# A transformer layer on one core: the first three feed-forward weight units quantized during the attention, and the last attention products placed between the first gate and up products

## The chip, the cores and the metric

The kernel runs on one core of a Trainium2 chip. The metric is the device time of one execution in microseconds (us), lower is better. The engines are called by the names of the profile: PE (TensorE), DVE (VectorE), ACT (ScalarE), POOL (GpSimd) and SP (SyncE, which here only starts transfers).

## What is computed

One pre-norm layer on 2048 tokens of width 1024, float32 in and out. First `x = x + attention(layernorm(x))`, where the attention mixes the 32 heads of each token with one another (scores are 32 x 32 for every token, not across tokens). Then `x = x + ffn(layernorm(x))`:

```
q, k, v = (h @ w.T + b).reshape(B, S, 32, 32)        # for wq, wk, wv
scores = einsum('bshd,bstd->bsht', q, k) / sqrt(32)
context = einsum('bsht,bstd->bshd', softmax(scores), v)
...
dq = NF4_CODE[searchsorted(bounds, w / absmax)] * absmax   # blocks of 64, for w1, w2, w3
h = silu(x @ dq1.T) * (x @ dq2.T)
return h @ dq3.T                                     # w1, w2: 2752 x 1024; w3: 1024 x 2752
```

So every feed-forward weight is rounded to one of 16 levels of its block of 64 before it is used, and that rounding is computed in the kernel.

## The kernel before

**Stages.** A first stage (to about 62 us) turns the three projection weights and splits them into a high and a low float16 part. The attention then takes the tokens in 16 tiles of 128, one `step` each (n = 0 to 15; steps 2 to 13 run in a loop of two). Step n projects tile n (`project_one`, 96 products of 512 columns on PE) and, between these, does the small products of tile n-1: 32 scores (`score_part`, L1048) and 32 products with V (`mix_part`, L1061), each against a block-diagonal stationary matrix, `q_diag` or `p_diag`. ACT fills these matrices (`place`, L934), DVE does the softmax, transposes and evacuations, POOL the residual, the reciprocal roots and the low halves. The normalized result of tile n-2 is split in two float16 halves (`halve2`, `low2`), transposed by DMA (`turn_high2`, `turn_low2`) and stored. Beside this DVE looks at all of w1, w2, w3 (`look_at`) for the largest value of each block of 64. `tail` finishes tile 15, whose scores and context have no projection left to hide behind.

**Feed-forward.** 22 tiles of the hidden dimension go in 11 rounds of two. A round first makes gate and up products (`gate_up`, tile p = 0 and 1, four blocks `sb_` of 512 tokens each, 24 products each for gate and for up), then 16 `down` tiles of 12 products. It needs six weight units of 128 x 1024; unit v of a round is UNIT[v], so the first six are w1 tile 0, w2 tile 0, w1 tile 1, w2 tile 1, w3 tile 0, w3 tile 1. A unit costs a division by the block maxima (POOL, `divide` L1378), 14 comparisons (ACT, `compare` L1497, into a ring of int8 signs), 14 multiply-adds (DVE, `sum_steps` L1633, in PSUM banks 0 and 1), a fifteenth comparison and two more passes on POOL (`step_apart`, `times_absmax`), the high half (ACT, `high_half` L1520), the low half (POOL, `low_half` L1410), and two DMA transposes (`turn` L1310). Between its sums DVE also makes the hidden values (`hidden_value` L1659) and adds the down products (`add_down` L1712). Three units are ahead at any time. The order on each engine is written out by hand; each engine runs its instructions in that order and waits at semaphores.

**The passage.** The feed-forward programs are generators. In the last step and in `tail` the attention program of each engine calls `next(feed)` at chosen places and so puts pieces of the opening of the feed-forward between its own. Before the change units 0 and 1 are made here in another way: ACT and DVE compare against the 15 bounds (`early_signs` L1508, `early_compares` L1643), and PE adds the results up by products with diagonal matrices of the level steps (`early_sums` L1861, 4 products for each of 15 levels and 2 units, with the scores and the context of tile 15 put between them); POOL makes these matrices (L1472), and DVE scales the sums (`early_codes` L1650). Unit 2 goes the usual way through DVE. The first gate product (L1804, which waits for unit 0) comes when all of that is done:

```
            early_sums(0, 0, 2)
            score = yield
            early_sums(0, 2, 7, score)
            early_sums(0, 7, LEVELS)
            early_sums(1, 0, 5)
            mix = yield
            early_sums(1, 5, 10, mix)
            early_sums(1, 10, LEVELS)
            yield
            pe.wait_ge(rounded, EARLY + 1)
            rounds(pe, body)
```

The x2 tokens that the gate products read are loaded back from DRAM (`load_tokens`, L1340) in blocks of 512; block 3 holds tiles 12 to 15.

## Time and profile before

| | |
|---|---|
| median of 3 runs | 1966.15 us (1963.84 to 1967.97) |
| profiled execution | 1965.0 us |
| its span, first to last instruction | 1963.1 us |
| mean granted TensorE clock | 0.995 |
| PE busy | 1911.5 us, 97% |
| DVE busy | 1738.3 us, 89% |
| ACT busy | 1477.6 us, 75% |
| POOL busy | 1192.4 us, 61% |
| first score product / end of the last projection | 90.1 us / 549.0 us |
| first gate product | 598.5 us |

Busy time is summed over an engine's instructions; the matmuls are pipelined, so each is shown longer (0.38 us) than the distance to the next. The idle time of an engine stands in square brackets, with what ended it. The profiled execution took 1.9 us more than its span.

### The profile page before, as it was taken

How to read it: one execution, taken by the hardware profiler on the slowest of the kernel's cores; microseconds unless marked ns; L12 is line 12 of the kernel's file. 1: busy time of each engine (PE TensorE's matmuls, PEld its weight loads, DVE VectorE, ACT ScalarE, POOL GpSimd, SP SyncE). 2: the span in 40 equal slices, each digit the busy share in tenths (PEclk: the TensorE clock that was granted, in tenths of full speed). 3: DMA queues.
4: the chain of work that ended last, by engine and by line, in shares of the span. 5: the costliest groups of instructions: out<-in, count | busy, mean ns of one | idle time of the engine just before them, and what ended most of it. 6: DMA issues, size and time to landing. Idle time of an engine off the chain costs nothing. (4 is left out here: it accounts for less than half of the span.)

```text
span 1963.1 us, 31165 instructions
## 1 busy us (share of the span) xinstructions
PE 1911.5 (97%) x10444; PEld 1062.7 (54%) x10444; DVE 1738.3 (89%) x1853; ACT 1477.6 (75%) x1672; POOL 1192.4 (61%) x715
## 2 busy tenths in 40 slices
PE   6899999999988989999999999999999999999998
PEld 6588888888854434444444444444444444444443
DVE  6788888888887999999999999999999999999982
ACT  7253443534486979899898998989989889898883
POOL 0211211112146787787887978879788797786975
PEclk9999999999999999999999999999999999999999
DMA  9335555455348512121221221212212212122114
GB/s 311 108 108 172 160 156 185 142 169 155 92 150 241 177 45 58 44 64 43 48 59 43 52 55 43 64 43 48 59 43 55 52 43 64 43 46 57 38 28 183
DMA packets 253803, 183.78 MB, mean 94 GB/s; under 512 B 177840, under 2 KB 220848, under 8 KB 253744
## 3 DMA queue, kind: packets, MB, share of 16 engines
q1 hardware_dynamic: 220144, 168.33, 30.6%
q10 hardware_dynamic: 33600, 14.69, 3.0%
q8 instruction: 34, 0.56, 0.1%
q14 instruction: 25, 0.20, 0.0%
HBM read 115.34 MB, written 25.17 MB: 72 GB/s over the span
## 5 line engine op out<-in xcount | busy, mean ns | idle before, releaser
L1633 DVE SCALAR_TENSOR_TENSOR bank<-signs,bank 128x1024 f32<-128x1024 int8 (+2 forms) x761 | 926.5, 1217 | 53.4 <-ACT signs L1497 25.6
L1497 ACT ACTIVATE signs<-w_nat,compare_bias 128x1024 int8<-128x1024 f32 (+2 forms) x896 | 959.1, 1133 | 5.3 <-POOL w_nat L1378 3.0
L1804 PE MATMUL bank<-x2T_hi,w12T_hi 128*128 128x512 f16 x1376 | 522.1, 379 | 7.7 <-DMA w12T_lo<-half 5.1
L1806 PE MATMUL bank<-x2T_hi,w12T_lo 128*128 128x512 f16 x1376 | 522.3, 380 | 0.0
L1805 PE MATMUL bank<-x2T_lo,w12T_hi 128*128 128x512 f16 x1376 | 522.2, 379 | 0.0
L1020 PE MATMUL bank<-wT_hi,xT_hi 128*128 128x512 f16 x768 | 293.2, 382 | 2.4 <-PEq L325 2.4
L1020 PE MATMUL bank<-wT_hi,xT_lo 128*128 128x512 f16 x768 | 293.1, 382 | 0.0
L1831 PE MATMUL bank<-w3T_hi,hT_hi 128*128 128x512 f16 x672 | 255.3, 380 | 8.9 <-DMA w3T_lo<-half 3.7
L1833 PE MATMUL bank<-w3T_hi,hT_lo 128*128 128x512 f16 x672 | 255.5, 380 | 0.0
L1832 PE MATMUL bank<-w3T_lo,hT_hi 128*128 128x512 f16 x672 | 255.4, 380 | 0.0
L1423 POOL TENSOR_TENSOR acc<-acc,hidden 128x512 f32<-128x512 f32 x176 | 221.0, 1271 | 39.8 <-ACT hidden L1546 39.0
L1390 POOL TENSOR_SCALAR step_part<-w_nat 128x1024 f32<-128x1024 f32 (+1 forms) x64 | 230.5, 3602 | 14.3 <-POOL w_nat L1403 7.4
L1804 PEld LDWEIGHTS bank<-x2T_hi,w12T_hi 128*128 128x128 f16 x1376 | 134.8, 98 | 171.5 <-issue 3.7
L1806 PEld LDWEIGHTS bank<-x2T_hi,w12T_lo 128*128 128x128 f16 x1376 | 134.7, 98 | 162.7 <-issue 0.7
L1805 PEld LDWEIGHTS bank<-x2T_lo,w12T_hi 128*128 128x128 f16 x1376 | 134.8, 98 | 162.5 <-issue 0.8
L1399 POOL TENSOR_TENSOR w_nat<-w_nat,step_part 128x1024 f32<-128x1024 f32 (+1 forms) x64 | 149.8, 2341 | 103.2 <-DVE w_nat L1633 103.2
L1546 ACT ACTIVATE hidden<-bank,un_scale 128x512 f32<-128x512 f32 x176 | 120.2, 683 | 112.0 <-PE bank L1833 66.1
L972 ACT ACTIVATE probs<-probs 128x512 f32<-128x512 f32 x32 | 20.2, 630 | 218.5 <-DVE probs L877 218.1
L1069 PEld LDWEIGHTS bank<-vT,p_diag 128*128 128x128 f32 x1024 | 169.0, 191 | 14.8
L1057 PEld LDWEIGHTS bank<-kT,q_diag 128*128 128x128 f32 x1024 | 169.0, 191 | 14.7
L1712 DVE SCALAR_TENSOR_TENSOR acc<-bank,un_scale,acc 128x512 f32<-128x512 f32 x176 | 131.3, 746 | 33.8 <-PE bank L1829 22.6
L1410 POOL TENSOR_TENSOR half<-w_nat,half 128x1024 f16<-128x1024 f32 (+1 forms) x66 | 139.7, 2116 | 29.7 <-ACT half L1520 29.7
(143 smaller groups left out, 2596.8 us busy)
## 6 DMA issues: line engine op xcount, KB each, us to landing
ff_raw<-in_L_ffn_w SPq DMA_DIRECT2D x63, 512.0 KB, 4.1
w_nat<-in_L_ffn_w SPq DMA_DIRECT2D x63, 512.0 KB, 3.9
x_nat<-in_L_attn_hidden_states SPq DMA_DIRECT2D x16, 512.0 KB, 5.0
x_res<-in_L_attn_hidden_states SPq DMA_DIRECT2D x16, 512.0 KB, 4.4
x<-x_res SPq DMA_DIRECT2D x16, 512.0 KB, 3.9
acc<-x SPq DMA_DIRECT2D x4, 2048.0 KB, 8.3
out<-acc SPq DMA_DIRECT2D x16, 512.0 KB, 2.7
w_raw<-in_L_attn_wq SPq DMA_DIRECT2D x8, 512.0 KB, 7.1
```

The source lines that it names most:

```text
L1020: ins = nc.tensor.matmul(to, x, w, start=j == 0, stop=j == len(passes) - 1)
L1057: ins = nc.tensor.matmul(scores[:, t], q_diag[:, t], kT[:, t // 2, :, t % 2], start=True, stop=True)
L1390: nc.gpsimd.tensor_scalar(step_part[0:rows, 0:cols], w_nat[0:rows, slot, 0:cols], float(BOUNDS[APART]), 2 * HALF_STEP[APART], ALU.is_gt, A ...
L1423: nc.gpsimd.tensor_tensor(acc[:, st, BANK:], acc[:, st, BANK:], hidden[:, st % 2], ALU.add).then_inc(summed, 1)
L1497: nc.scalar.activation(signs[0:rows, ring(v, k), 0:cols], w_nat[0:rows, v % SLOTS, 0:cols], ACT.Sign, scale=COMPARE[SUMMED[k]][0], bias=co ...
L1633: V.scalar_tensor_tensor(to, part, HALF_STEP[SUMMED[k]], before, ALU.mult, ALU.add).then_inc(sign_used, 1)
L1804: nc.tensor.matmul(dst, hi, x2T_hi[:, toks, c], start=c == 0, stop=False)
L1805: nc.tensor.matmul(dst, hi, x2T_lo[:, toks, c], start=False, stop=False)
L1806: last = nc.tensor.matmul(dst, lo, x2T_hi[:, toks, c], start=False, stop=c == C - 1)
L1831: nc.tensor.matmul(dst, hT_hi[k, p, toks], w3T_hi[k, p, cols], start=p == 0, stop=False)
L1832: nc.tensor.matmul(dst, hT_hi[k, p, toks], w3T_lo[k, p, cols], start=False, stop=False)
L1833: last = nc.tensor.matmul(dst, hT_lo[k, p, toks], w3T_hi[k, p, cols], start=False, stop=p == GROUP - 1)
```

## The change

It makes units 0, 1 and 2 during steps 1 to 15, three of the 45 levels in each: POOL divides a unit once (`open_unit`), ACT compares and scales (`make_level`: two activations), POOL adds (`add_level`). PE and DVE have no part in it. To make room the two block-diagonal matrices become one (`diag`, halves of which hold q and the probabilities in turn), `qkv` becomes one row buffer, and the halves of the weights get a buffer of their own from the start. In the last step POOL and ACT scale and split units 0 and 1, and unit 2 in the tail. All of `early_signs`, `early_compares`, `early_sums`, `early_codes`, the diagonal matrices and DVE's sums for unit 2 go. DVE's work on the scales (`look_at_scales`, `set_scales`, the reciprocals) moves from the last step and the tail to the end of step 14 and into step 15. PE goes on from the last projection with the first gate products; the scores of tile 15 sit one behind each of products 0 to 31, its context behind products 40 to 71 (of 96: gate of block 0, gate of block 1, up of block 0, up of block 1), in PSUM banks 6 and 7. Tiles 14 and 15 of x2 are transposed straight into place instead of going through DRAM. ACT and POOL no longer loop over the steps. Unit 3's sums are spread over DVE's tail.

```
-            for diag in (q_diag, p_diag):
-                pool.memset(diag[:], 0.0).then_inc(diag_zero, 1)
+            pool.memset(diag[:], 0.0).then_inc(diag_zero, 1)
...
+            def add_level(n, i):
+                at = (n - 1) * STEP_LEVELS + i
+                v, k = divmod(at, LEVELS)
+                if k > 0:
+                    pool.wait_ge(level_ready, at + 1)
+                    ...
+                    nc.gpsimd.tensor_tensor(codes[v], codes[v], level, ALU.add).then_inc(level_added, 1)
...
+            def make_level(n, i):
+                ...
+                if adds_before(at) > 0:
+                    act.wait_ge(level_added, adds_before(at))
+                nc.scalar.activation(level, ratio, ACT.Sign, scale=COMPARE[k][0], bias=compare_bias[:, k:k + 1]).then_inc(level_sign, 1)
+                act.wait_ge(level_sign, at + 1)
+                nc.scalar.activation(codes[v] if k == 0 else level, level, ACT.Copy, scale=HALF_STEP[k]).then_inc(level_ready, 1)
...
@@ attention, scalar, step @@
                 if attend:
+                    make_level(n, 0)
                     exponential(n, 0)
                     place_probs(n, 0, end)
...
                     place_probs(n, 1, end)
...
+                if attend:
+                    make_level(n, 1)
                 if project:
-                    place(q_diag, qT[:].rearrange("p t h u -> p t u h"), q_placed)
+                    place_q(n, 0, attend)
...
+                if attend:
+                    make_level(n, 2)
+                if project:
+                    place_q(n, 1, attend)
...
@@ attention, gpsimd, step @@
                 if end:
                     residual(n - 2)
+                if feed:
+                    next(feed)
                 if normalize:
                     inv_std(pool, n + 1)
                 if end:
                     inv_std2(n - 2)
+                if attend:
+                    add_level(n, 0)
                 if feed:
                     next(feed)
                 if end:
                     low2(n - 2)
+                if attend:
+                    add_level(n, 1)
                 if feed:
                     next(feed)
+                if attend:
+                    add_level(n, 2)
+                if n * STEP_LEVELS % LEVELS == 0 and n + 1 < T:
+                    open_unit(n * STEP_LEVELS // LEVELS)
+                if ahead:
+                    next(ahead)
...
@@ attention, vector, tail @@
                 evacuate(T - 1, 1, None, 2, 1)
                 turn_v(T)
+                moments2(T - 2)
                 next(feed)
                 center(T, 0)
+                norm2(T - 2)
+                flip_probs(T, 0, True)
+                next(feed)
                 center(T, 1)
...
@@ attention, sync, tail @@
                 sp.wait_ge(projected, 6 * T)
+                next(feed)
                 sp.wait_ge(evacuated, 6 * T)
-                sp.wait_ge(x2_out, 32 * (T - ST_BLOCK + 1))
                 next(feed)
                 store_x1(T - 2)
...
+            def turn_tokens(n):
+                sp.wait_ge(x2_hi_done, n + 1)
+                sp.dma_start_transpose(x2T_hi[:, n], x2_half[:]).then_inc(x2_turned, 16)
+                sp.wait_ge(x2_lo_done, n + 1)
+                sp.dma_start_transpose(x2T_lo[:, n], x2_low).then_inc(x2_turned, 16)
...
+                        for at, (m, sb_) in enumerate(((0, 0), (0, 1), (1, 0), (1, 1))):
+                            gate_up(r, 0, sb_, P, (m,), True, 3 * C * at)
...
+                def attend_last(slot):
+                    if slot < QUAD:
+                        score_part(T, True, slot, slot + 1)
+                    elif MIX_FROM <= slot < MIX_FROM + QUAD:
+                        mix_part(T, slot - MIX_FROM, slot - MIX_FROM + 1)
```

DVE's pieces of the feed-forward, in their new order (step 14's end; then five places in step 15; then the tail): `look_at_scales`; `floor_scales`; `set_scales`; `first_reciprocals`, `scale_absmax`; `invert(2, 11)`; `invert(11, 22)`; sum 0; sums 1 to 3; sum 4; sums 5 and 6; sums 7 to 9; `hidden_value(0, 0, 0)` and sums 10 and 11; `hidden_value(0, 0, 1)`; sums 12 to 15. POOL's in step 15: the square root of the scales; `early_times(0)`, `early_times(1)`, `early_low(0)`, `early_low(1)`; `divide(0, 3)`. ACT's: `early_high(0)`, `early_high(1)` between `place_probs(15, 0)` and the second exponential. SP loads block 0 of the x2 tokens in step 15, behind the transposes and the store of tile 13, and blocks 1 and 2 at the two waits of its tail. `place_q(n, half)` waits for the context of the same half (`context_done`), since both use `diag`.

## Rows read from the trace of the kernel before

**Rows 1.** The page: busy time of the engines, and GpSimd over forty slices.

```profile
PE 1911.5 (97%) x10444; PEld 1062.7 (54%) x10444; DVE 1738.3 (89%) x1853; ACT 1477.6 (75%) x1672; POOL 1192.4 (61%) x715
...
POOL 0211211112146787787887978879788797786975
```

**Rows 2.** Timeline, PE, 549 to 703: start, us, line, work, idle before.

```profile
556.27 1.01 PE L1861 MATMUL bank<-w3T_hi,w12T_hi 128*128 128x512 f16 x2 [7.31 <-issue]
...
598.49 0.39 PE L1804 MATMUL bank<-x2T_hi,w12T_hi 128*128 128x512 f16 x1 [2.63 <-DVE w_nat L1650]
...
650.49 0.39 PE L1804 MATMUL bank<-x2T_hi,w12T_hi 128*128 128x512 f16 x1 [2.64 <-DMA w12T_lo<-half]
...
702.36 0.39 PE L1831 MATMUL bank<-w3T_hi,hT_hi 128*128 128x512 f16 x1 [3.69 <-DVE acc L1712]
```

**Rows 3.** Windows of PE: us, busy (count), granted clock, DMA share, GB/s.

```profile
555.00:560.00 5.00, 3.73 (x12) 0.57 1.05 398
```

**Rows 4.** Timeline of a looped attention step (starts 427.35, next 458.00), PE, ACT, DVE, POOL.

```profile
427.35 0.30 PE L1057 MATMUL bank<-kT,q_diag 128*128 128x32 f32 x2
...
458.00 0.30 PE L1057 MATMUL bank<-kT,q_diag 128*128 128x32 f32 x2
...
473.77 0.30 PE L1069 MATMUL bank<-vT,p_diag 128*128 128x32 f32 x2
...
479.48 0.30 PE L1069 MATMUL bank<-vT,p_diag 128*128 128x32 f32 x2
...
477.25 1.26 ACT L937 ACTIVATE p_diag<-flipped 32x512 f32<-32x512 f32 x2
...
466.58 0.80 DVE L279 TENSOR_SCALAR x_nat<-x_nat,mean_var,rstd 128x1024 f32<-128x1024 f32 x1
...
464.72 0.55 POOL L721 TENSOR_TENSOR rstd<-var_eps,power 128x1 f32<-128x1 f32 x1 [1.20 <-DVE var_eps L267]
```

**Rows 5.** Groups by line: name, shapes, count, busy us, mean ns.

```profile
L1399 POOL TENSOR_TENSOR w_nat<-w_nat,step_part 128x1024 f32<-128x1024 f32 x61 | 143.9, 2358 | 96.3 <-DVE w_nat L1633 96.3
...
L937 ACT ACTIVATE p_diag<-flipped 32x512 f32<-32x512 f32 x128 | 80.3, 628 | 50.1 <-DVE flipped L892 29.7 <-issue 19.3
...
L1520 ACT ACTIVATE half<-w_nat 128x1024 f16<-128x1024 f32 x63 | 66.1, 1050 | 10.1 <-DVE w_nat L1650 5.3 <-POOL w_nat L1403 4.8
...
L1508 ACT ACTIVATE hT_hi<-w_nat,compare_bias 128x1024 f16<-128x1024 f32 x7 | 7.7, 1133 | 0.0
```

**Rows 6.** Timeline around 582.5, DVE and POOL.

```profile
582.67 2.41 DVE L883 TENSOR_SCALAR x_res<-x_res,mean_var,rstd 128x1024 f32<-128x1024 f32 x1
...
582.41 2.13 POOL L1410 TENSOR_TENSOR half<-w_nat,half 128x1024 f16<-128x1024 f32 x1 [4.55 <-ACT half L1520]
```

**Rows 7.** Timeline, DVE: the two long reciprocals.

```profile
548.62 2.52 DVE L1678 RECIPROCAL inv_absmax<-inv_absmax 128x384 f32<-128x384 f32 x1
...
588.64 3.75 DVE L1678 RECIPROCAL inv_absmax<-inv_absmax 128x576 f32<-128x576 f32 x1
```

**Rows 8.** DMA issues: KB each, median us from issue to landing.

```profile
x<-x_res SPq DMA_DIRECT2D x16, 512.0 KB, 3.9
...
x2T_lo<-x_lo_dram SPq DMA_DIRECT2D x4, 1024.0 KB, 8.4
...
w12T_lo<-half SPq DMA_TRANSPOSE x44, 3.1
```

**Rows 9.** Timeline, POOL and DVE, 601 to 702.

```profile
601.67 2.38 POOL L717 TENSOR_TENSOR x_res<-x_res,flipped 128x1024 f32<-128x1024 f32 x1 [5.67 <-DMA x_res<-in_L_attn_hidden_states]
...
609.59 0.81 DVE L883 TENSOR_SCALAR x_res<-x_res,mean_var,rstd 128x1024 f32<-128x1024 f32 x1 [2.53 <-DMA x<-x_res]
...
648.68 0.75 DVE L1659 SCALAR_TENSOR_TENSOR hidden<-bank,un_scale,hidden 128x512 f32<-128x512 f32 x1 [1.15 <-ACT hidden L1528]
...
701.56 0.74 DVE L1712 SCALAR_TENSOR_TENSOR acc<-bank,un_scale,acc 128x512 f32<-128x512 f32 x1
```

**Rows 10.** Windows of all engines: PE, PEld, DVE, ACT, POOL busy (count).

```profile
760.00:800.00 40.00, 40.00 (x187) 18.19 (x186) 38.93 (x35) 38.12 (x41) 30.55 (x16) 1.00 0.23 53
```

571 lines of the change are left out of this document (284 added, 287 removed).

## The prediction, made before the result was seen

> **What bounds the kernel now.** I read the page first. PE is busy for 97% of the span [rows 1], so only two things can shorten the kernel: PE work that goes, and the stretches in which PE waits. POOL's slices are at 0 to 2 tenths up to the feed-forward [rows 1]: that is the room which the change uses. The timeline of PE then shows where it waits. It runs without a gap through the attention to 549.0 us, sits idle for 7.3 us to 556.3, and starts the first gate product at 598.5 [rows 2]. Between lie the 120 summing products and tile 15's scores and context. After that come, among shorter ones, waits of 2.6 and 3.7 us [rows 2], and further on none: in a 40 us window of a later round PE has 187 products, one per 0.214 us, and DVE is busy for 38.9 of the 40 [rows 10]. So from the first down products on PE and DVE are nearly equal, and neither can make up time; what the passage gains or loses stays to the end. The wait at 702.4 has DVE behind it [rows 2]: at that point DVE is the later one. From the fourth hidden value (648.68) to the first addition of a down product (701.56) DVE runs 38 sums and four hidden values with hardly a gap, 52.9 us [rows 9]. The change touches none of these. Small pieces that have no row of their own (a softmax step, a transpose, an issue) are my estimates from the same timeline. I cost the change as the shift of that fourth hidden value, `hidden_value(0, 0, 3)`. It needs the up product of token block 3, thus the x2 of tile 15, and the DVE work ahead of it.
>
> **Attention steps 1 to 14.** Each gets two ScalarE activations per level, 1.13 us (Sign, with a 16-bit output) and 1.05 us (Copy) [rows 5], three times: 6.6 us, and three POOL additions of 2.36 us [rows 5]: 7.1 us. Both engines have that room. What matters is the order. The second half of the probabilities is in place at 477.25 + 1.26 = 478.5, and PE reads it at 479.5 [rows 4]: 1.0 us of slack. No new ACT work stands ahead of it after the step's beginning. But the first `add_level` follows the reciprocal root of 464.72 + 0.55 = 465.3 and runs to 467.6, over the x normalization on DVE at 466.58, which takes 0.80 us alone [rows 4]. Such an instruction suffers: the x2 normalization at 582.67 took 2.41 us while POOL worked from 582.41 to 584.54, and ended 0.5 us after it [rows 6], against 0.81 us in [rows 9]. The Trainium skill (GPSIMD Reference, section 1, Specifications) states that VectorE instructions in a two-port mode or with two SBUF inputs contend with GpSimd; the row agrees for the first kind, and no row of the second kind is used here. So the normalization ends at 468.2 instead of 467.4, everything behind it on DVE and ACT comes 0.8 us later, and 0.2 us of slack is left: no wait, taken as 0, though closely. The bound below is 0. The one above is an addition that starts just before the normalization: 2.36 + 0.5 - 0.80 = 2.1 us late, less 1.0 us slack, 1.1 us for each of 14 steps, 15 us.
>
> The single `diag` forces an order: q of the next tile can be placed only when the context of the same half is done. The first half is done at 479.5, the second at 485.2. A half takes 4 x 0.63 = 2.5 us [rows 5], with 2.2 us of `make_level` before each: first half at about 484, second at about 490. PE's steps start 30.7 us apart (427.35, 458.00), so it wants them at 488.7 and 5.7 us later, at 494.4. Slack 4 us: cost 0. One buffer for q, k and v changes no order on DVE: 0. The missing `memset` and the shorter first stage are off PE's path: 0. Straight instead of looped code on ACT and POOL: between 0 and a few tenths of a microsecond per step, taken as 0, since nothing on these engines is late by less than the slack.
>
> **Step 15.** Here DVE gets more: `set_scales` with its small operations (2 us), `scale_absmax` (1 us), the two reciprocals of 2.5 and 3.75 us [rows 7], and `look_at_scales` moves ahead of the step. By the order of the code the reduction over partitions on POOL now comes before tile 13's residual, and both before the centring: the first half of the probabilities comes about 3 us late. The second half has `set_scales`, `early_high` twice on ACT, and three DVE operations held by POOL's `early_times` and `early_low` (2 us each, back to back) before it: about 6 us more. I add 9 us: PE's projections end at 558 instead of 549. Bounds: 0 and 12.
>
> **The start of the gate products.** They need unit 0 (split and transposed by about 546, hidden) and token block 0. SP issues its load behind tile 13's transposes and store, at about 550.5, and the low half, issued half a microsecond behind the high one, lands 8.4 us later [rows 8]: 559.4, taken as 559.5. So of the 9 us of step 15 only 1.5 us count, the rest lies beside the load, as PE's idle 7.3 us do now. A wait that long also costs clock: the granted clock was 0.57 in 555 to 560 [rows 3]; with the shorter waits I take no loss (bound above 2 us).
>
> **The opening.** 24 products take 5.2 us; a small product behind each adds (479.48 - 473.77) / 16 - 0.214 = 0.14 us [rows 4], 9.2 us for all 64, which were also done before. Undisturbed, the context of tile 15 would be done 25 us after 559.5. Two waits come in. The x2 normalization of tile 14 stands before `flip_probs` on DVE and waits for `store_x1(14)`, which SP issues at 563.6 (by the 13 us that DVE's added work and waits put on tile 14's transpose, 548 before), behind the loads of blocks 1 and 2: about 8 us to landing in place of 3.9 [rows 8], the same queue as a block load. That makes the first half of the probabilities 3 us late (ready 576), the second 1.5 us more, with sums 1 to 4 ahead of it on DVE. Context done: 588.8. Then the chain of the last tile: weighing and transpose 2 us, residual 2.4, and from its end to the normalization 5.5 us as in [rows 9] (604.05 to 609.59, the store that must land); normalization 0.8, high half 1.05 [rows 5], low half 2.1 [rows 6], issue and DMA transpose 1.2 + 3.1 [rows 8]: 588.8 + 18.1 = 606.9. The roundtrip through DRAM that followed is gone. PE meanwhile: last up product 594, block 2 604.4, then a wait of 2.5 us, block 3 until 617.3; silu and hidden value: 618. DVE has then finished sums 0 to 15 of unit 3 and 4 and eight more (by 613), since unit 2's 14 sums, ten comparisons and two scalings left it; it is no later than PE.
>
> **The sum.** 648.7 - 618.0 = 30.7 us earlier. The waits before the down products come again as they are, since the same DVE chain sets them. 1965.0 - 30.7 = 1934.3 us for the profiled execution; the median of the runs was 1.15 us above that execution, so 1935.5, rounded to 1935 us. The own range of this case is 1924 (nothing in step 15 and the store at 3.9 us: 10 us less) to 1944 (12 us in step 15, clock lost, store and last chain 3 us later each).
>
> **Rivals.** (1) POOL holds DVE in every step, the bound above: 1935 + 15 = 1950. For it speaks the 0.2 us of slack; against it that the addition starts 1.3 us before the normalization [rows 4], so most of it is over. Any lateness of 0.5 us per step already gives 1942. Chance 0.2, 1944 to 1956. (2) DVE isn't the bound of the passage, so that PE's own work sets the end: from 598.5 to its last product PE has about 1343 us of products besides its waits; 559.5 + 9.2 + 1343 + 8 to the end of the execution gives 1920. For it speaks that DVE loses some 35 us of work in the tail; against it the gapless 52.9 us of [rows 9]. Chance 0.13. (3) Slower: the shared `diag`. If ACT's chain from the context to q (two `make_level`, each waiting for POOL, then the placing) runs over its slack of 4 us, PE stands at the scores of each step. It decides from 30.7 / 14 = 2.2 us per step beyond the slack, so 6 us more than I count; at 9 us more it would be 1935 + 70 = 2005. Chance 0.04. (4) The early units are not what held the gate products, and tile 15's chain alone keeps the end within 0.2%: the fourth hidden value would have to stay at 645 to 652, which only a wait of 30 us could do. Chance 0.02.
>
> **Numbers.** Forecast 0.61, rivals 0.2, 0.13, 0.04 and 0.02. About 0.2% of the time (4 us) is what a measurement of this kernel can tell from no change. Faster than that: 0.61 + 0.2 + 0.13 = 0.94; within 0.02; slower 0.04. The range that leaves out no more than 2 in 10 reaches to most of both faster rivals: 1920 to 1951.
>
> **What would show it.** Right: no wait of PE in steps 1 to 14 and the same distance of 30.7 us between their starts; waits of some us before the context products of step 15; first gate product near 559, its releaser the token load; `hidden_value(0, 0, 3)` near 618; 52.9 us from there to the first addition; 187 products per 40 us later. Wrong: idle time on PE before score or context products of each step with ACT's placing as releaser (rivals 1 and 3); a gate product before 552; a distance to the first addition below 50 us (rival 2).

## The result and the profile after

The changed kernel takes 1948.17 us (median of 4 runs, 1946.46 to 1950.49), the kernel before 1964.99 us (4 runs, 1961.58 to 1967.97): ratio 0.9917, 95% interval 0.9905 to 0.993. The forecast was 1935 us within 1920 to 1951. The sign is right and the range holds it, but about 13 us of the expected 30 did not come. The profiled execution took 1950.5 us (span 1948.4, against 1963.1 before).

In these texts, lines of code after the change are those of the changed kernel; `L1154` is the context product (before: L1069), `L1883` gate and up, `L1002` the placing into `diag`, `L766` `add_level`, `L772` the residual addition, `L949` the x2 normalization, `L1788` `add_down`.

PE's waits first, as in [rows 2] (timeline of PE, 540 to 690: start, length, line, work, idle before and what ended it):

```profile
544.58 0.60 PE L1154 MATMUL bank<-vT,diag 128*128 128x32 f32 x2 [10.51 <-ACT diag L1002]
...
555.97 0.64 PE L1154 MATMUL bank<-vT,diag 128*128 128x32 f32 x2 [3.34 <-ACT diag L1002]
...
571.82 0.39 PE L1883 MATMUL bank<-x2T,w12T 128*128 128x512 f16 x1 [3.45 <-DMA x2T<-x_lo_dram]
...
589.36 0.38 PE L1154 MATMUL bank<-vT,diag 128*128 128x32 f32 x2 [2.34 <-ACT diag L1002]
...
636.81 3.65 PE L1883 MATMUL bank<-x2T,w12T 128*128 128x512 f16 x10 [2.65 <-DMA w12T<-half]
...
687.14 0.61 PE L1911 MATMUL bank<-w3T_hi,hT_hi 128*128 128x512 f16 x1 [3.72 <-DVE acc L1788]
```

The first gate product is at 571.82, where it was at 598.49; the forecast had 559.5. Ahead of it stand two waits in step 15, 13.9 us together, and one for the token load. Around them the clock is low: the granted clock was 0.50, which is the level of 1.2 GHz, in the 5 us around the first wait, and 0.57 around the second (windows of all engines; the number behind POOL's is the clock, then DMA share and GB/s):

```profile
540.00:545.00 5.00, 0.42 (x3) 0.46 (x4) 4.83 (x11) 3.06 (x5) 3.89 (x2) 0.50 0.00 0
...
555.00:560.00 5.00, 4.04 (x18) 3.59 (x19) 4.96 (x6) 4.91 (x7) 1.75 (x1) 0.57 1.05 211
```

Up to step 14 everything went as forecast. DVE's x normalization starts beside a level addition and takes 1.58 us, 0.8 more than in [rows 4], and no wait of PE follows (DVE, then POOL, in the looped step):

```profile
466.33 1.58 DVE L276 TENSOR_SCALAR x_nat<-x_nat,mean_var,rstd 128x1024 f32<-128x1024 f32 x1
...
465.00 2.37 POOL L766 TENSOR_TENSOR codes<-codes,w12T 128x1024 f32<-128x1024 f32 x1
```

The trouble begins behind step 14, on POOL (timeline of POOL, 516 to 550):

```profile
516.79 2.38 POOL L766 TENSOR_TENSOR codes<-codes,w12T 128x1024 f32<-128x1024 f32 x1 [2.52 <-ACT w12T L1045]
524.89 0.39 POOL L1568 PARTITION_ALL_REDUCE top_all<-top  x1 [5.72 <-issue]
532.38 2.37 POOL L772 TENSOR_TENSOR x_res<-x_res,flipped 128x1024 f32<-128x1024 f32 x1 [7.11 <-issue]
534.72 0.59 POOL L1571 TENSOR_TENSOR top_all<-pow,power 128x1 f32<-128x1 f32 x1
...
541.11 4.21 POOL L1556 TENSOR_TENSOR w12T<-w12T,inv_first 128x1024 f32<-128x1024 f32 x2 [1.56 <-DVE inv_first L1778]
```

The reduction over the partitions itself takes 0.39 us. But POOL stands for 5.72 us ahead of it and for 7.11 us behind it, "issue", that is, for nothing that the profile shows. Before the change the residual addition of tile 13 was at 518.45 and the reduction at 529.32, with 7.44 us of the same stand behind it, beside other work. Now `ahead` puts the reduction first, so the residual addition comes 13.9 us later, and DVE stands for it, with the centring of the scores queued behind. The stand ahead of the reduction is not all lost: its input, DVE's `top`, is ready only at 521.92, so 3.0 us of the 5.72 lie behind that. What POOL does in the two stands no run shows. (Timeline of DVE:)

```profile
521.74 0.18 DVE L1750 TENSOR_REDUCE top<-ff_raw 128x1 f32<-128x22 f32 x1
...
534.78 1.29 DVE L258 BATCH_NORM_STATS2 stats<-x_res 128x6 f32<-128x512 f32 x2 [9.30 <-POOL x_res L772]
...
541.14 0.71 DVE L958 STREAM_TRANSPOSE flipped<-probs 128x512 f32<-128x512 f32 x1
...
546.86 5.85 DVE L1782 TENSOR_SCALAR absmax<-absmax,w_scale 128x352 f32<-128x352 f32 x3
552.64 0.70 DVE L958 STREAM_TRANSPOSE flipped<-probs 128x512 f32<-128x512 f32 x1
...
584.87 0.81 DVE L949 TENSOR_SCALAR x_res<-x_res,norm_row 128x1024 f32<-128x1024 f32 x1 [4.06 <-DMA x<-x_res]
```

The second flip stands behind `scale_absmax`, three instructions that took 0.40 us each before and 5.85 us together here, beside POOL's `early_low` and `low2`.

The stands delay the codes of units 0 and 1 as well: the root, which the scales need, is at 534.72, the multiplication at 541.11, and unit 0's low half ends at 548.15. The token load follows from that (timeline of POOL, 545 to 548, then SP's queue, 548 to 574):

```profile
545.59 2.56 POOL L1560 TENSOR_TENSOR x_nat<-w12T,x_nat 128x1024 f16<-128x1024 f32 x1 [0.28 <-ACT x_nat L1606]
```

```profile
548.24 0.33 SPq L1362 DMA_DIRECT2D w_nat<-in_L_ffn_w  x1
548.69 3.35 SPq L1425 DMA_TRANSPOSE w12T<-x_nat  x2
...
555.84 2.66 SPq L1425 DMA_TRANSPOSE w12T<-x_nat  x2
...
560.83 0.92 SPq L1416 DMA_DIRECT2D x2T<-x_hi_dram  x1
561.80 1.11 SPq L1416 DMA_DIRECT2D x2T<-x_lo_dram  x1
...
573.62 0.35 SPq L701 DMA_DIRECT2D x<-x_res  x1
```

SP waits until 548.2 for the low half of unit 0 (12.8 us in the list of its waits, ended by POOL's L1560). It also waits for the projections of q, but these had ended at 530.3, and those of k, which the token load needs, end at 552.3. From 548.2 it issues thirteen transfers in one piece, and the token load of block 0 is the last of them, at 560.83 where the forecast had 550.5. So neither of PE's two waits in step 15 holds the token load; the late codes do.

Later on: the fourth hidden value is at 632.35 (forecast 618, before 648.68 [rows 9]) and the first addition of a down product at 686.34 (before 701.56), 54.0 us later:

```profile
632.35 0.75 DVE L1735 SCALAR_TENSOR_TENSOR hidden<-bank,un_scale,hidden 128x512 f32<-128x512 f32 x1 [3.03 <-ACT hidden L1624]
...
686.34 0.74 DVE L1788 SCALAR_TENSOR_TENSOR acc<-bank,un_scale,acc 128x512 f32<-128x512 f32 x1
```

The rounds behind are as they were, 187 products in 40 us [rows 10]; the busy line of the page shows the 120 summing products gone and ACT and POOL fuller [rows 1]:

```profile
PE 1892.1 (97%) x10324; PEld 1058.0 (54%) x10324; DVE 1722.9 (88%) x1833; ACT 1552.3 (80%) x1792; POOL 1277.0 (66%) x724
```

```profile
760.00:800.00 40.00, 40.00 (x187) 18.13 (x186) 38.84 (x35) 36.88 (x40) 27.93 (x14) 1.00 0.24 54
```

### The profile page after: what moved, and what is told of

It reads as the page before. It is cut to its first block, busy times and chain, and to the rows that moved or that the text cites. A ratio compares the mean times of both kernels' runs of the same rounds, so it can differ in the third digit from the quotient of the medians.

```text
span 1948.4 us, 30908 instructions
## 1 busy us (share of the span) xinstructions
PE 1892.1 (97%) x10324; PEld 1058.0 (54%) x10324; DVE 1722.9 (88%) x1833; ACT 1552.3 (80%) x1792; POOL 1277.0 (66%) x724
## 4 chain that ended last, share of the span: by engine, by line
PE 64%; DVE 0%; issue 0%; ACT 0%; DMA 0%; POOLq 0%; SPq 0%; POOL 0%; DVEq 0%
PE bank L1883 41%; PE bank L1911 7%; PE bank L1912 7%; PE bank L1913 7%; PE bank L1909 0%; PE bank L1908 0%; DVE bank L1727 0%; DMA w3T_lo<-half 0%; ACT hidden L1642 0%; POOLq L154 0%; DVE bank L1725 0%; DVE w_nat L1727 0%; SPq L1386 0%; ACT half L1614 0%; ACT signs L1601 0%
## 5 line engine op out<-in xcount | busy, mean ns | idle before, releaser
L1883 PE MATMUL bank<-x2T,w12T 128*128 128x512 f16 x4128 | 906.4, 380 | 6.6 <-DMA x2T<-x_lo_dram 3.5
L1883 PEld LDWEIGHTS bank<-x2T,w12T 128*128 128x128 f16 x4128 | 410.3, 99 | 488.0 <-DMA x2T<-x_lo_dram 3.9
L1481 POOL TENSOR_SCALAR step_part<-w_nat 128x1024 f32<-128x1024 f32 (+2 forms) x63 | 226.9, 3601 | 10.6 <-POOL w_nat L1494 7.4
L1490 POOL TENSOR_TENSOR w_nat<-w_nat,step_part 128x1024 f32<-128x1024 f32 (+2 forms) x63 | 147.5, 2341 | 91.9 <-DVE w_nat L1727 91.8
L1154 PEld LDWEIGHTS bank<-vT,diag 128*128 128x128 f32 x1024 | 175.7, 196 | 33.4 <-issue 13.8
L1142 PEld LDWEIGHTS bank<-kT,diag 128*128 128x128 f32 x1024 | 171.6, 192 | 15.2
L1154 PE MATMUL bank<-vT,diag 128*128 128x32 f32 x1024 | 159.5, 238 | 16.2 <-ACT diag L1002 16.2
L1788 DVE SCALAR_TENSOR_TENSOR acc<-bank,un_scale,acc 128x512 f32<-128x512 f32 x176 | 131.4, 747 | 34.2 <-PE bank L1909 22.5
L1142 PE MATMUL bank<-kT,diag 128*128 128x32 f32 x1024 | 156.5, 234 | 0.0
L1501 POOL TENSOR_TENSOR half<-w_nat,half 128x1024 f16<-128x1024 f32 (+2 forms) x63 | 133.3, 2116 | 25.1 <-ACT half L1616 25.1
L1104 PEld LDWEIGHTS bank<-wT_hi,xT_lo 128*128 128x128 f16 x768 | 115.3, 150 | 31.3 <-issue 1.6
```

What stands on the lines that cost most here:

```text
L1104: ins = nc.tensor.matmul(to, x, w, start=j == 0, stop=j == len(passes) - 1)
L1142: ins = nc.tensor.matmul(scores_of(n)[:, t], diag[:, t], kT[:, t // 2, :, t % 2], start=True, stop=True)
L1154: ins = nc.tensor.matmul(context_of(n)[:, t], diag[:, t], vT[:, t // 2, :, t % 2], start=True, stop=True)
L1481: nc.gpsimd.tensor_scalar(step_part[0:rows, 0:cols], w_nat[0:rows, slot, 0:cols], float(BOUNDS[APART]), 2 * HALF_STEP[APART], ALU.is_gt, A ...
L1490: nc.gpsimd.tensor_tensor(w_nat[0:rows, slot, 0:cols], w_nat[0:rows, slot, 0:cols], step_part[0:rows, 0:cols], ALU.add).then_inc(step_adde ...
L1883: last = nc.tensor.matmul(dst, w, x[:, toks, c], start=c == 0 and i == 0, stop=c == C - 1 and i == 2)
```

## The experiments

All start from the changed kernel. Each profile's clock starts at a slightly different point of the execution, so times of different kernels are compared as distances from one row, the moments of x on DVE in step 13 (L258, `stats<-x_nat`, at 460.84 in the changed kernel). "Turn", "gate" and "addition" are the distances from there of SP's issue of unit 0's transposes, of the first gate product and of the first `add_down`. The runs were made in five sets, in which the kernel before had medians of 1962.9 to 1965.0 us, so between sets a difference of medians below some 2 us says nothing; the distances do not have this fault.

| kernel | time, us | context waits of step 15 | wait for the gate | turn | gate | addition |
|---|---|---|---|---|---|---|
| changed | 1948.2 | 10.5 + 3.3 | 3.5 | 87.9 | 111.0 | 225.5 |
| e1, reduction is a copy | 1939.5 | 0.3 + 5.4 | 3.0 | 77.6 | 100.4 | 215.1 |
| e2, reduction twice | 1947.3 | 11.0 + 3.5 | 3.4 | 88.4 | 111.3 | 225.8 |
| e3, scaling later | 1949.3 | 10.3 + 0 | 9.8 | 87.7 | 110.4 | 224.1 |
| e4, normalization later | 1947.4 | 10.0 + 3.2 | 3.1 | 87.3 | 110.3 | 224.0 |
| e5, tokens of block 0 first | 1949.7 | 10.2 + 2.2 | 0 | 93.4 | 103.9 | 228.9 |
| e6, no levels | 1962.7 | 6.5 + 3.1 | 4.7 | 83.9 | 106.7 | 220.6 |
| e7, reduction behind the residual | 1952.5 | 0 + 0 | 28.0 | 94.1 | 116.2 | 229.9 |
| e9, store ahead of tokens | 1942.8 | 10.2 + 2.2 | 6.4 | 87.5 | 110.4 | 220.7 |
| e12, both chains | 1944.2 | 0 + 0 | 18.5 | 84.7 | 106.6 | 220.9 |
| e13, both chains, tokens | 1941.8 | 0 + 0 | 8.8 | 84.7 | 97.0 | 218.6 |
| e14, levels of 8 columns | 1942.8 | 6.7 + 3.1 | 4.8 | 84.0 | 106.9 | 219.5 |
| e16, and hidden value first | 1939.7 | 0 + 0 | 8.4 | 84.7 | 96.5 | 217.8 |

Wherever SP's order up to the tokens of block 0 is that of the changed kernel (all but e5, e13 and e16), the gate comes 21.9 to 23.1 us behind the turn, whatever PE waited for in step 15.

**Is it the stand of POOL?**

```diff
-            nc.gpsimd.partition_all_reduce(top_all[:], top[:], P, ALL_MAX).then_inc(ff_max_all, 1)
+            nc.gpsimd.tensor_copy(top_all[:], top[:]).then_inc(ff_max_all, 1)
```

> The maximum over the partitions, which GpSimd takes at the end of step 14, is replaced by a plain copy of the same tile on GpSimd (this leaves out that maximum, so the scales of the first two units are those of each partition's own rows). Theory, that GpSimd stands for about 7 us between the reduction and its next ordinary instruction: the residual addition of block 13 starts about 7 us and more earlier (now 532.4, then near 523 to 525), VectorE's idle stretch of 9.3 us ahead of the row centring is gone, TensorE's wait of 10.5 us at 544.6 shrinks to under 3, and the time is about 1938 to 1941 us (ratio to the kernel before about 0.987). Rival, that the wait is VectorE's and ScalarE's added load of step 15 (inversions, scales, high halves): the residual addition moves, but the wait at 544.6 keeps 6 us or more and the time stays above 1944.

Measured: 1939.5 us (1938.47 to 1940.09), ratio 0.9883 (0.9867 to 0.99). Both stands are gone (timeline of POOL):

```profile
520.24 0.19 POOL L1568 COPY top_all<-top 128x4 f32<-128x4 f32 x1 [2.81 <-DVE top L1750]
520.38 2.40 POOL L772 TENSOR_TENSOR x_res<-x_res,flipped 128x1024 f32<-128x1024 f32 x1
```

The residual addition starts 10.3 us earlier by distance, the first wait is gone, and the first gate product comes 10.6 us earlier, as the turn of unit 0 comes 10.2 us earlier. The second wait grew to 5.4 us: PE, at full clock, reaches it sooner, and the 5.85 us of the scaling are still there. The theory's time was right. This puts 8.7 us on the reduction and its stands by the medians, 6.7 by the ratios to the kernel before, and 10.4 at the first addition.

**How often does POOL stand?**

```diff
+            nc.gpsimd.partition_all_reduce(top_all[:], top[:], P, ALL_MAX).then_inc(ff_first_all, 1)
+            pool.wait_ge(ff_first_all, 1)
             nc.gpsimd.partition_all_reduce(top_all[:], top[:], P, ALL_MAX).then_inc(ff_max_all, 1)
```

> The maximum over the partitions is taken twice in a row on GpSimd, same result. If the pause of about 7 us belongs to each such reduction, residual addition of block 13 starts 12 to 14 us later than in the changed kernel (near 545) and the time rises by about 12, to 1960. If the pause belongs to the return from a reduction to ordinary instructions, only the second reduction's own time is added, some 1 to 6 us, and the time rises by no more than that. Rival, that GpSimd's pause does not set TensorE's wait: the time does not move.

Measured: 1947.31 us (1945.97 to 1949.24), as the changed kernel.

```profile
523.86 0.39 POOL L1569 PARTITION_ALL_REDUCE top_all<-top  x1 [5.78 <-issue]
524.34 0.37 POOL L1571 PARTITION_ALL_REDUCE top_all<-top  x1
531.82 2.36 POOL L772 TENSOR_TENSOR x_res<-x_res,flipped 128x1024 f32<-128x1024 f32 x1 [7.10 <-issue]
```

The second reduction starts 0.48 us after the first. So the price is at the changes, from ordinary instructions to the reduction and back, and not in the reduction: two in a row pay it once. The time alone doesn't separate this from the rival, which had no change either; e1 does.

**The second wait alone.**

```diff
             first_reciprocals()
-            scale_absmax()
             yield
             invert(2, FT // 2)
+            scale_absmax()
```

> One instruction group is moved: VectorE's scaling of the maxima (three instructions, 5.85 us in the changed kernel, 0.40 us each in the kernel before) goes behind the flips of the second half of the probabilities and the second inversion. Theory, that its 5.85 us are all that makes the wait of 3.34 us at 556.0, and that GpSimd's running additions, not the scaling itself, make them: the wait is gone, the three instructions take another time where they stand now, and the kernel gains 2 to 3.5 us (about 1945.5). Rival, that the inversion behind it is held in its place, since whatever stands there meets the same additions: the wait stays above 2 us and the time is that of the changed kernel.

Measured: 1949.34 us (1946.28 to 1950.61), no gain. The wait is gone, as the theory had it; the three instructions took 4.07 us in their new place, so they are held there as well. But the gate starts only 0.6 us earlier by distance, and PE's wait there grew from 3.5 to 9.8 us. Both the theory's gain and the rival's mechanism were wrong: the wait was real and did not matter. PE's projections end 6.9 us earlier by distance, but the turn of unit 0 and the token load behind it stay where they were.

**Both waits, by order alone.** POOL does the residual addition and the standard deviation of tile 13 ahead of the reduction; DVE's scales and ACT's high halves go behind the scores' work. In POOL's step:

```diff
                 if end:
                     residual(n - 2)
-                if feed:
-                    next(feed)
                 if normalize:
                     inv_std(pool, n + 1)
                 if end:
                     inv_std2(n - 2)
+                if feed:
+                    next(feed)
+                    next(feed)
                 if attend:
                     add_level(n, 0)
...
-                if ahead:
-                    next(ahead)
```

> Same work in another order at the passage from step 14 to 15. GpSimd: residual addition and standard deviation of block 13 go ahead of the reduction over the partitions and the root behind it. VectorE: floor of the scales, scales and first reciprocals go behind the evacuations of step 15 that they stood ahead of, the inversions behind them, the scaling of the maxima last. ScalarE: the high halves of the first units go just ahead of the placing of q of tile 15. Theory, that the two waits of 10.5 and 3.3 us at 544.6 and 556.0 come from what was queued there (the residual addition behind GpSimd's stand, the flips behind a scaling that took 5.85 us): both together shrink to under 4 us, the slow-clock stretches between them go, the first gate product comes 8 to 13 us earlier, and the time is 1936 to 1941. Rival, that the same work is only delayed and then holds the turns of the early codes or the last projections: the first gate product gains under 5 us and the time is 1943 to 1950.

Measured: 1952.48 us (1951.67 to 1953.44), ratio 0.9942 (0.9925 to 0.9958), slower than the changed kernel. PE stands nowhere in step 15, and then for 28 us:

```profile
575.55 0.61 PE L1884 MATMUL bank<-x2T,w12T 128*128 128x512 f16 x1 [28.02 <-DMA x2T<-x_lo_dram]
```

The rival was right, and more than right:

```profile
532.67 0.39 POOL L1569 PARTITION_ALL_REDUCE top_all<-top  x1 [5.54 <-issue]
540.37 0.59 POOL L1572 TENSOR_TENSOR top_all<-pow,power 128x1 f32<-128x1 f32 x1 [7.31 <-issue]
...
546.52 4.37 POOL L1557 TENSOR_TENSOR w12T<-w12T,inv_first 128x1024 f32<-128x1024 f32 x2 [1.14 <-DVE inv_first L1779]
```

The root, now the first instruction behind the stand, comes 7.1 us later by distance than in the changed kernel, the early codes with it, and SP starts turning unit 0 at 553.5, 6.3 us later by distance. So two things must be done before the gate: PE's own projections, and a chain of reduction, root, scales, codes, turn and token load. In the changed kernel the projections end at 568.4 and the tokens have landed 3.4 us later, so the chain of the codes decides. That explains both this run and the one before: e3 and e7 brought the projections forward by 6.9 and 19.4 us, which gained nothing, and e7 made the other chain 6.3 us longer; the copy of e1 brought both forward by 10 us. Between q's projections and SP there is no link that matters: they end at 69.4 by distance in every kernel here.

**The order on SP.** First the tokens of block 0 ahead of the turns:

```diff
+            sp.wait_ge(projected, 6 * (T - 1) + 4)
+            load_tokens(0)
             turn_early(0)
             yield
             turn_early(1)
             load(0, 4, P)
             yield
-            load_tokens(0)
             yield
```

> On SyncE's queue the token load of the first feed-forward block goes ahead of the two early turns of the codes, as soon as the last projections have read the buffer. Theory, that the wait of 3.45 us ahead of the first gate product is this load alone, queued behind the turns: the wait goes, the gate starts about 3.5 us earlier and the time falls by 3 to 3.5 us (about 1945). Rival, that the gate then waits for its weights, whose turn is now issued later: the wait stays between 1 and 3.5 us under another name, and the time moves by under 2 us.

Measured: 1949.74 us (1948.96 to 1951.53). The wait is gone and the gate 7.1 us earlier, then PE waits for the tokens of block 1:

```profile
578.43 0.61 PE L1884 MATMUL bank<-x2T,w12T 128*128 128x512 f16 x1 [8.03 <-DMA x2T<-x_lo_dram]
```

In SP's queue the turn of unit 0 now starts 5.5 us later by distance, mostly because SP waits 4.9 us for the projections of k, which PE's first wait holds up; and it took 7.13 us to issue in place of 3.35, behind the 2 MB of tokens. Everything behind it, the load of the residual row of tile 14 too, moved back (from 559.24 to 564.57, which by distance is 8.3 us). Neither theory named the place; the rival's size was nearer.

Then the normalization of tile 14, from both ends: once moved behind the flips on DVE (and `halve2` behind the placing on ACT), once by an earlier store.

```diff
                 center(T, 0)
-                norm2(T - 2)
                 flip_probs(T, 0, True)
+                norm2(T - 2)
                 next(feed)
```

> In the closing step VectorE's normalization of block 14 and ScalarE's halving behind it are moved behind the last probabilities' flips and placing. Theory, that the wait of 2.34 us at 589.4 comes from VectorE being held until the residual row of block 14 has come back from memory: the wait goes and the time falls by up to 2.3 us against the changed kernel (about 1946). Rival, that the last scores-to-context chain has slack elsewhere or that the later turn of block 14 delays the last context's companions: no change, or 0 to 2 us slower.

Measured: 1947.44 us (1946.45 to 1948.19). The first half of the last context goes on without a wait, but the second waits 2.76 us: on DVE the normalization still waits 2.94 us for the store, and the centring of the second half is behind it. The wait changed its place.

```diff
             load_tokens(1)
             yield
-            load_tokens(2)
             yield
+            load_tokens(2)
```

> On SyncE's queue the token load of block 2 (two transfers of 1 MB) goes behind the store of the residual row of block 14 instead of ahead of it. Theory, that VectorE's 4.06 us at 584.9 and TensorE's 2.34 us at 589.4 come from that store's landing of 11.2 us behind the transfers ahead of it: the store lands in 6 to 8 us, the normalization of block 14 starts 3 to 4 us earlier, the wait of 2.34 us is gone, and the time falls by 1.5 to 2.5 us against the changed kernel (about 1946). Rival, that the queue order does not matter since all engines' transfers share the same 400 GB/s: landing stays over 10 us and nothing moves; or that block 2's tokens then come late: a new wait at block 2.

Measured: 1942.81 us (1940.62 to 1943.89), ratio 0.9894 (0.9878 to 0.9911): 5.4 us better than the changed kernel, more than the theory had; 4.8 us at the first addition. No wait is left at the last context, and the fourth hidden value comes 4.6 us earlier by distance. Of these 0.6 us are there at the gate, 2.3 us are the wait, and the rest fits the clock: the 10 us behind the wait ran at 0.84 before and the corresponding ones at 1.00 here (windows, changed kernel, then e9):

```profile
590.00:600.00 10.00, 10.00 (x71) 9.06 (x72) 8.14 (x11) 9.82 (x13) 2.92 (x2) 0.84 0.63 133
```

```profile
590.00:600.00 10.00, 10.00 (x68) 6.93 (x67) 7.93 (x9) 6.64 (x8) 1.68 (x1) 1.00 0.24 46
```

**Do the levels cost the attention anything?**

```diff
-                nc.scalar.activation(level, ratio, ACT.Sign, scale=COMPARE[k][0], bias=compare_bias[:, k:k + 1]).then_inc(level_sign, 1)
-                act.wait_ge(level_sign, at + 1)
-                nc.scalar.activation(codes[v] if k == 0 else level, level, ACT.Copy, scale=HALF_STEP[k]).then_inc(level_ready, 1)
+                act.sem_inc(level_sign, 1)
+                act.sem_inc(level_ready, 1)
...
-                    nc.gpsimd.tensor_tensor(codes[v], codes[v], level, ALU.add).then_inc(level_added, 1)
+                    pool.sem_inc(level_added, 1)
```

> The levels of the three early units are left out of the attention: ScalarE's comparison and scaling and GpSimd's addition, 42 of each or more, are replaced by bare counts (the codes of these units are then the raw weights, so the output is not the reference's). Theory, that they cost the attention steps nothing: the distance between the steps' starts stays 30.7 us, step 15 is the same but for ScalarE's and GpSimd's own additions there, and the time is within 4 us of the changed kernel, 1944 to 1948. Rival, that GpSimd's additions hold VectorE and with it TensorE in each step: up to 15 us less, 1933 to 1940.

Measured: 1962.74 us (1957.75 to 1965.44, 10 runs), which neither side expected: less work, 14.6 us slower. The attention is not at fault, and the first addition even comes 4.9 us earlier by distance (220.6). The time goes in the rounds behind, where PE waits once per round for DVE's hidden value, eight times and 14.9 us in all (the last of them, 1.15 us, is in the changed kernel too, 1.14), and ACT shows this in seven of them (timelines of PE and of ACT):

```profile
1058.98 0.39 PE L1910 MATMUL bank<-w3T_hi,hT_hi 128*128 128x512 f16 x1 [1.98 <-DVE hidden L1734]
...
1101.19 3.23 ACT L1600 ACTIVATE signs<-w_nat,compare_bias 128x1024 int8<-128x1024 f32 x3 [4.06 <-issue]
```

The changed kernel has no such stand. The profile counts 64 transfers of the kind "instruction" on queue q14 here, 28 in the changed kernel; in a round with a stand there are five, in the same stretches of the changed kernel none. To see if it comes from the place of ACT's code, every instruction was put back with 8 of 1024 columns:

```diff
-                nc.scalar.activation(level, ratio, ACT.Sign, scale=COMPARE[k][0], bias=compare_bias[:, k:k + 1]).then_inc(level_sign, 1)
+                nc.scalar.activation(level[:, 0:8], ratio[:, 0:8], ACT.Sign, scale=COMPARE[k][0], bias=compare_bias[:, k:k + 1]).then_inc(level_sign, 1)
...
-                    nc.gpsimd.tensor_tensor(codes[v], codes[v], level, ALU.add).then_inc(level_added, 1)
+                    nc.gpsimd.tensor_tensor(codes[v][:, 0:8], codes[v][:, 0:8], level[:, 0:8], ALU.add).then_inc(level_added, 1)
```

> The levels of the three early units are taken over 8 of 1024 columns only, with every instruction kept (the codes of the other columns stay the raw weights). It stands against the run without the levels, which got slower, 1962.7 us, through eight waits of 2 us in the rounds after 900 us, each behind a stand of ScalarE of 4.1 us that ends on nothing the profile shows. Theory, that these stands come from where ScalarE's loop lies among its instructions, and not from the work left out: with the instructions kept they are gone, ScalarE shows none of 4.1 us, and the time is 1939 to 1946, some 5 us under the changed kernel's. Rival, that the missing work or the changed codes make them: the time is again above 1955.

Measured: 1942.82 us (1941.28 to 1944.32). The stands are gone, and q14 has 28 instruction transfers again. The levels cost the attention steps nothing that can be measured: from the first score product to the one at 427 it is 337.04 us with the levels, without them and with the small ones, 337.07 before the change. They do cost something behind step 14. There POOL has been idle for 8.55 us when DVE's `top` comes, and the reduction starts 0.13 us behind it instead of 3.0 (timeline of POOL; in e6 it is the same after 15.09 us):

```profile
519.85 0.39 POOL L1568 PARTITION_ALL_REDUCE top_all<-top  x1 [8.55 <-DVE top L1750]
527.05 2.39 POOL L772 TENSOR_TENSOR x_res<-x_res,flipped 128x1024 f32<-128x1024 f32 x1 [6.80 <-issue]
```

So, by these traces, the stand ahead of a reduction runs from the last ordinary instruction, and time that POOL is idle anyway hides it. In the changed kernel that instruction is the last level of step 14. Without its length the reduction comes 2.8 us earlier by distance than in the changed kernel, the gate 4.0 us (106.9) and the first addition 6.0; where the last 2 us come from is not shown.

**Both chains at once.** POOL: residual addition, reduction, root, standard deviation, then the codes of units 0 and 1, with tile 13's low half right behind unit 0's. DVE: all of step 15's scores first, then the scales, then the x2 normalization of tile 13. ACT: the high halves behind both placings. SP: e9's store. In POOL's step:

```diff
                 if end:
                     residual(n - 2)
                 if feed:
                     next(feed)
+                    next(feed)
                 if normalize:
                     inv_std(pool, n + 1)
                 if end:
                     inv_std2(n - 2)
+                if feed:
+                    next(feed)
+                    low2(n - 2)
                 if attend:
                     add_level(n, 0)
```

> All work kept, two chains freed together. GpSimd does the residual addition of block 13 first, then the reduction, the root, the standard deviation, the multiplication of the first two units and the low half of unit 0; VectorE does the whole scores side of step 15 ahead of the scales, and normalizes block 13 behind them; ScalarE takes the high halves behind both placings; SyncE stores the residual row of block 14 ahead of block 2's tokens. Theory, that the gate waits for the later of two chains, of which the run with the reordered reduction freed the scores and delayed the codes by 7 us: here the codes are ready as in the changed kernel or up to 2 us later and TensorE stands under 3 us ahead of the context products, so that the first token load goes out 3 to 6 us earlier than in the changed kernel; the time is 1934 to 1940, against 1942.8 of the store's move alone. Rival, that code turns and loads on SyncE's queue (12 us of issues in one piece) set the gate whatever comes before: the gate starts within 2 us of the changed kernel's and the time is that of the store's move alone, 1941 to 1944.

Measured: 1944.18 us (1943.38 to 1944.6). PE stands nowhere in step 15, unit 0 is turned 3.1 us and the token load is issued 4.3 us earlier by distance than in the changed kernel, but of that nothing arrives at the first addition (220.9 against 220.7 of e9), as a new wait of 3.18 us at 603.46, ended by DVE's first hidden value, follows. The time is what the rival had; its reason is not, since the gate did move.

**The tokens of block 0 behind the turn of unit 0**, on top of the last kernel:

```diff
             turn_early(0)
+            sp.wait_ge(projected, 6 * (T - 1) + 4)
+            load_tokens(0)
             yield
             turn_early(1)
             load(0, 4, P)
             yield
-            load_tokens(0)
             yield
```

> As the run with both chains freed, and the tokens of block 0 are loaded right behind the turn of unit 0, ahead of block 13's own transposes and the turn of unit 1. Theory, that with the last projections over early the tokens of block 1 are no longer late (they cost 8 us where only the tokens of block 0 were moved): the gate starts another 2 to 5 us earlier, no wait follows at block 1, and the time is 1930 to 1937. Rival, that the transfers share one bandwidth (about 400 GB/s in this stretch), so that what goes ahead takes from what is behind: a wait of 3 us or more at the up products or at block 1, and no gain against the run without it.

Measured: 1941.83 us (1941.31 to 1942.31), 2.4 us better. The gate comes 9.7 us earlier than in e12, and most of it is given back: 6.13 us of wait at block 1, as the rival had it, and again 3.18 us at the hidden value:

```profile
573.30 0.61 PE L1885 MATMUL bank<-x2T,w12T 128*128 128x512 f16 x1 [6.13 <-DMA x2T<-x_lo_dram]
...
601.25 38.97 PE L1885 MATMUL bank<-x2T,w12T 128*128 128x512 f16 x172 [3.18 <-DVE hidden L1737]
```

**What is late next.**

```diff
+            hidden_value(0, 0, 0, P)
             sum_steps(0, opening_steps[7:10], FULL)
             yield
-            hidden_value(0, 0, 0, P)
             sum_steps(0, opening_steps[10:12], FULL)
```

> As the run with both chains freed and the tokens of block 0 moved (1941.8 us), and VectorE takes the first hidden value ahead of three sums instead of behind them and the moments of block 15. Theory, that the new wait of 3.18 us at 601.25, which VectorE's first hidden value ends, is what gives back the earlier gate: the first hidden value comes 4 to 5 us earlier (near 595), that wait is gone, the first addition into the result comes 2 to 4 us earlier and the time is 1938 to 1940. Rival, that VectorE's and ScalarE's chain of comparisons and sums is the bound of this passage in any order: the wait goes but another of the same size stands before the fourth hidden value or before the down products, and the time stays within 1.5 us of 1941.8.

Measured: 1939.73 us (1939.2 to 1943.45), ratio 0.9887 (0.9871 to 0.9904). The first hidden value is at 593.38 and the wait is gone, but one of 2.36 us ("issue") stands at 609.35, so the rival has a part in it. The addition gains only 0.8 us by distance and the medians 2.1, so by the trace less is shown than by the times; the ranges of e13 and e16 overlap. It is the best version with all the work kept: 23.5 us under the kernel before (1963.2 in the same runs), and 8.4 us under the changed kernel by the medians, 5.9 by the ratios.

## Why the prediction was right and where it was wrong

- **Bound and direction.** Right: the passage sets the end, and the rounds behind neither gave nor took (the end moved by 14.5 us in the profiled executions, the first addition by 15.2, the fourth hidden value by 16.3).
- **Steps 1 to 14 at 0.** Right, with its small parts: normalization held by 0.8 us, no wait, and the same distances with the levels and without. Rival 1, whose time of 1950 is near the result, is refuted as a mechanism. Its rule, that GpSimd contends with VectorE instructions in a two-port mode or with two SBUF inputs (the Trainium skill, GPSIMD Engine Reference, section 1, Specifications), agrees with the trace: the normalization took 1.58 us beside a full level addition and 0.80 us in e6 and e14, where that is missing or tiny. But no wait followed; and the second wait of step 15, which `scale_absmax` with its 5.85 us made, could be removed (e3) without a gain.
- **The early codes.** Here is the step that failed. The prediction had unit 0 "split and transposed by about 546, hidden", and the token load issued "at about 550.5"; the reduction's new place was priced only as probabilities "about 3 us late", from no row. The trace of before shows POOL's stands around the same instruction, 5.7 us ahead and 7.4 us behind, at 529.32 and 537.15, and the prediction did not cost them as a thing that moves with the reduction. In the run, unit 0's low half was ready only at 548.15 and the token load was issued at 560.83 (560.83 - 550.5 = 10.3 us late); from the issue of its low half to the gate it took 10.0 us instead of 8.4. With the reduction as a copy, the load went out at 548.40 on that kernel's clock, 550.1 on the changed kernel's: the forecast value.
- **Step 15 on PE.** Wrong by the same step, but without effect on the time. The first wait was 10.5 us instead of 3, the second 3.3 instead of 6, so 13.9 in place of 9 with 12 as the bound above. The projections ended near 568.4, not 558: 19.4 us later than before, and the 5.5 us beyond the waits fit the slow clock around them, which the prediction put at nothing. "Of the 9 us only 1.5 us count" had the right picture, a wait that lies beside the load: even the 19.4 us did not reach the gate.
- **Opening.** 60.5 us from the first gate product to the fourth hidden value, forecast 58.5. The store of tile 14 landed in 11.2 us, taken as 8, and PE waited 2.3 us for it, plus clock; the prediction had 3 us and another 1.5 for the second half.
- **Passage to the first addition.** 54.0 us, taken as 52.9. Together: 1934.3 + 12.3 (gate) + 2.0 + 1.1 = 1949.7, and the profiled execution took 1950.5.
- **Rival 2** (PE alone sets the end) was not reached: even with the gate at 96.5, e16 ends near 1940, and DVE's chain of sums and hidden values comes next. Rival 3, the shared `diag`, costs nothing: no wait stood before a score product. The bound above of 1944 for the likeliest case was too low by the stand. That the range holds the result is luck in part: it reached to 1951 for the sake of rival 1, which did not happen.

What stays open: how much of e16's 2.1 us is real, and whether an order of SP's queue exists that serves the turns, block 0 and block 1 at once. A maximum over the partitions by another way than POOL's reduction, which e1 says is worth up to 8.7 us, was not tried, and neither was the reduction at a place where POOL is idle anyway.

## What to carry to other kernels

Moving an instruction moves everything that stands around it in the trace, the idle time marked "issue" too: before the change those 7.4 us lay beside other work, and at the new place they lay on the path. Before you shorten a wait, look up what ended the last wait ahead of the thing that you want earlier, down to the queue that issues the load; two waits of 13.9 us together could be removed here and the kernel became slower, since the tokens waited for the codes and not for PE. And when work is taken out of a looped kernel as an experiment, put a small instruction in place of each, or the code's place in the program is changed with it.

## What the runs showed of the hardware

- POOL's reduction over partitions takes 0.4 us. Behind it POOL stands for 6.6 to 7.4 us until its next ordinary instruction, in all thirteen traces that have it. In eleven of them it starts 5.5 to 6.2 us after the ordinary instruction ahead of it; in e14 and e6, where POOL had been idle for 8.55 and 15.09 us, it starts 0.13 and 0.14 us after its input. Two in a row pay this once (e2), and a copy in its place has neither stand (e1).
- With 90 instructions fewer on ACT (1702 against 1792) ahead of its loop, ACT stood for 4.0 us once per round in seven rounds, 28.2 us in all, and the kernel lost some 15 to 20 us (1962.7 against 1942.8 with the same instructions kept small). The profile shows 64 transfers of the kind "instruction" on queue q14 instead of 28. The Trainium skill (Runtime: NRT & Kernel Launch, Instruction fetch mechanics) says that a taken branch whose target isn't among the loaded pages makes the engine fetch the page first; the pair of runs agrees with that, and doesn't show the reason: only the place of the code, the stands and the transfers were seen to go together.
- An SP queue that turns tiles and loads tokens is slowed by its own loads: the turn of unit 0 took 3.35 us to issue alone and 7.13 us behind 2 MB of tokens.
